# A state-space and mixture-of-experts kernel: states of four channel groups summed side by side, D * u as products with diagonals

## The reference

```
xi, z = split(x @ in_w.T);  u = silu(causal_conv4(xi) + conv_b)
dt, B, C = split(u @ x_w.T, [8, 24])
delta = softplus(dt @ dt_w.T + dt_b);  A = -exp(A_log)          # 256 channels x 16 states
h[t] = h[t-1] * exp(delta[t] * A) + delta[t] * u[t] * B[t]
y[t] = sum over the states of h[t] * C[t]  +  u[t] * D
out = (y * silu(z)) @ out_w.T
```

## Time and profile before

| | us |
|---|---|
| median of three runs (lowest, highest) | 963.63 (962.39, 965.27) |
| the profiled execution's own time | 960.58 |
| its span, first to last instruction | 958.7 |
| DVE busy | 883.0 |
| PE, POOL, ACT busy | 816.3, 801.6, 707.4 |
| mean granted clock of PE | 0.931 of 2.4 GHz |

### The profile page before, as it was taken

One profiled execution on the slowest core, in us unless ns is written; L12 is line 12 of the kernel. 1 busy time (PEld: TensorE's weight loads), 2 busy tenths in 40 slices (PEclk: granted clock), 3 DMA queues, 4 the chain that ended last, 5 costly groups with the idle time before them and its releaser, 6 DMA issues. The chain is left out here.

```text
span 958.7 us, 10740 instructions
## 1 busy us (share of the span) xinstructions
PE 816.3 (85%) x3009; PEld 327.2 (34%) x3009; DVE 883.0 (92%) x628; ACT 707.4 (74%) x1184; POOL 801.6 (84%) x451
## 2 busy tenths in 40 slices
PE   8787887796498998989898998989989899889577
PEld 5323322141133533435233443434434242223122
DVE  4979989998899999999899899998999999998986
ACT  4588774765468899887888889898788968574540
POOL 0468676999999999988798979998798999999993
PEclk9979989898799999999799999989999998889788
DMA  6676254332364647364453655654365444553300
GB/s 210 178 213 160 50 145 97 138 102 70 129 152 154 154 125 184 98 191 116 151 130 102 188 133 173 162 157 103 86 203 133 136 105 130 133 172 74 91 0 12
DMA packets 91452, 125.56 MB, mean 131 GB/s; under 512 B 8057, under 2 KB 62714, under 8 KB 87426
## 3 DMA queue, kind: packets, MB, share of 16 engines
q1 hardware_dynamic: 89346, 120.68, 46.0%
q0 software_dynamic: 2048, 4.20, 1.3%
HBM read 77.53 MB, written 14.29 MB: 96 GB/s over the span
## 5 line engine op out<-in xcount | busy, mean ns | idle before, releaser
L1314 POOL TENSOR_TENSOR hs<-hs,C_rep 128x1024 f32<-128x1024 f32 x250 | 585.0, 2359 | 70.6 <-DVE hs L1116 37.7
L1097 DVE TENSOR_TENSOR in_b<-in_b,B_rep 128x1024 f32<-128x1024 f32 x256 | 300.3, 1217 | 41.2 <-PE in_b L580 41.0
L917 ACT ACTIVATE dA<-delta_rep,A_sb 128x511 f32<-128x511 f32 x512 | 332.9, 713 | 1.7 <-DVE hs L1116 1.2
L604 PE MATMUL y<-hs,cst 128*32 128x512 f32 x1024 | 274.1, 656 | 32.2 <-POOL hs L1314 20.8
L1116 DVE TENSOR_TENSOR_SCAN hs<-dA,in_b 128x1024 f32<-128x1024 f32 x128 | 285.5, 2268 | 8.6 <-ACT dA L917 4.8
L1114 DVE TENSOR_TENSOR_SCAN hs<-dA,in_b 128x1024 f32<-128x1024 f32 x128 | 285.2, 2268 | 2.4 <-PE y L604 1.6
L580 PE MATMUL in_b<-du,cst 128*128 128x512 f32 x256 | 144.2, 646 | 29.8 <-DVE hs L1116 20.5
L604 PEld LDWEIGHTS y<-hs,cst 128*32 128x32 f32 x1024 | 52.5, 115 | 207.1 <-issue 165.5
L541 PE MATMUL front<-xpad,w_in 128*128 128x512 f32 x248 | 120.5, 610 | 2.4 <-ACT xpad L829 1.6
L926 ACT ACT_TABLE_LOAD x71 | 91.1, 1283 | 7.3 <-PE moe L732 4.7
L580 PEld LDWEIGHTS in_b<-du,cst 128*128 128x128 f32 x256 | 43.8, 197 | 96.4 <-issue 93.7
(11 more groups left out here) (144 smaller groups left out, 805.4 us busy)
## 6 DMA issues: line engine op xcount, KB each, us to landing
delta_rep<-tmpA SPq DMA_DIRECT2D x126, 256.0 KB, 4.4
C_rep<-dbc_scratch SPq DMA_DIRECT2D x16, 1024.0 KB, 7.4
B_rep<-dbc_scratch SPq DMA_DIRECT2D x15, 1024.0 KB, 5.2
gu_w<-in_gate_up SPq DMA_DIRECT2D x39, 384.0 KB, 3.3
dn_w<-in_down SPq DMA_DIRECT2D x39, 192.0 KB, 2.5
xs<-sorted_tokens SPq DMA_DIRECT2D x39, 64.0 KB, 3.9
sorted_ffn<-ys SPq DMA_DIRECT2D x39, 64.0 KB, 2.2
sorted_tokens<-up_f SPq DMA_DIRECT2D x9, 256.0 KB, 4.5
```

The lines of the kernel that those rows point to most:

```text
L604: i = e.matmul(Y[c * DD:(c + 1) * DD, :], sel, hs[:, (m + 2 * w + rh) % NH, r * L:(r + 1) * L], start=False, stop=(rh == 1 and r == RH - 1 ...
L917: i = e.activation(dA[:, m // 2 % NA, r * L + 1:(r + 1) * L], src, ACT.Exp, scale=A_sb[:, d, 2 * p + jj, r:r + 1])
L1097: e.tensor_tensor(to, in_b[:, 2 + 2 * odd, :].unsqueeze(1).broadcast_to([P, RH, L]), by, ALU.mult).then_inc(dve_mult, 1)
L1314: e.tensor_tensor(hs[:, m % NH, :], hs[:, m % NH, :], C_rep[:, u % 2, RH * rh:RH * rh + RH, :].rearrange("p r t -> p (r t)"), ALU.mult).th ...
```

## The change

- **Sums.** `sum_states` takes half a unit: four channel groups, each in its own 32 columns of the array, interleaved. A call has 8 products (16 instructions), one for even and one for odd steps, at steps 8i+12 and 8i+13. The ring hs has 13 slots.
- **D * u.** ACT's L899 is gone; PE's `skip` starts the bank Y with a product of a diagonal (`diag_D`, four of them, made by DVE in the head) and u.
- **Decays.** dA has four tiles of half a group; decay m waits for scan m-4. `delta_rep` has five single slots in place of three pairs.
- **dbc** lies in tmpB[:, 1], softplus' buffer; dt_out(v, 1) waits until it is stored.
- **Residual.** xn_in is gone: ACT's `residual` makes x + norm(x) from x_in with 4 activations, and one product adds it.
- **Order.** On every engine pieces are moved within a step or by some steps; one more product with C (step 180) is on DVE.

Before and after, cut to its core:

```diff
-NP = 3
-NA, NH = 3, 10
+NP, NR = 3, 5
+NA, NH = 4, 13
-CLEAR = 4
-WARM, WARM_PAUSE = 24, 7
+CLEAR = 3
+WARM, WARM_PAUSE = 24, 5
-C_ON_DVE = (41, 56, 217, 226, LAST - 2, LAST - 1)
+C_ON_DVE = (41, 56, 180, 217, 226, LAST - 2, LAST - 1)
...
-        dbc = sb("dbc", [NDBC, L])
-        delta_rep = sb("delta_rep", [P, NP, 2, L])
+        dbc = tmpB[0:NDBC, 1, :]
+        delta_rep = sb("delta_rep", [P, NR, L])
-        dA = sb("dA", [P, NA, R * L + 1])
+        dA = sb("dA", [P, NA, RH * L + 1])
...
# PE
+            def skip(i):
+                u, h = divmod(i, 2)
+                e.wait_ge(act_y, i)
+                e.wait_ge(act_xi, i + 1)
+                e.wait_ge(dve_diag, 4)
+                e.matmul(Y[:, :], diag_D[:, 2 * (u % 2) + h, :], xi[:, u % 2, h, :], start=True, stop=False,
+                         skip_group_check=True).then_inc(pe_skip, 1)
-            def sum_states(u, p, rh, groups=(0, 1)):
-                m = NSTEP * u + 4 * p
-                if m and p % 2 == 0 and rh == 0:
-                    e.wait_ge(act_D, 2 * u + p // 2)
+            def sum_states(u, h, rh, groups=(0, 1, 2, 3), signal=True):
+                m = NSTEP * u + 8 * h
                 wait_c(e, m + 2 * groups[-1] + rh)
                 for r in range(RH):
-                    for w in groups:
-                        c = (2 * p + w) % 4
-                        i = e.matmul(Y[c * DD:(c + 1) * DD, :], sel, hs[:, (m + 2 * w + rh) % NH, r * L:(r + 1) * L],
+                    for c in groups:
+                        i = e.matmul(Y[c * DD:(c + 1) * DD, :], sel, hs[:, (m + 2 * c + rh) % NH, r * L:(r + 1) * L],
...
-                for v in fronts(m, -11, -11):
+                for v in fronts(m, -10, -11):
                     x_proj(v)
-                for v in fronts(m, -10, -10):
+                for v in fronts(m, -10, -11):
                     dt_proj(v, 0)
-                for v in fronts(m, -9, -9):
+                for v in fronts(m, -9, -10):
                     dt_proj(v, 1)
-                for b in gathers(m, 6):
+                for b in gathers(m, 7):
                     if b < NB - LATE:
                         final_mm(b)
...
# ACT
+            def residual(b):
+                e.wait_ge(in_base, 16 * (b + 1))
+                for k in range(KB):
+                    o = e.activation(x_in[:, k, :], x_in[:, k, :], ACT.Identity, scale=root1[:, b, k:k + 1],
+                                     bias=shift[:, b, 0, k:k + 1])
+                o.then_inc(act_base, 1)
             def dt_out(v, h):
                 e.wait_ge(pe_dt, 2 * v + h + 1)
+                if h:
+                    e.wait_ge(out_dbc, 16 * (v + 1))
...
-                e.activation(Y[:, :], xi[:, u % 2, h, :], ACT.Copy,
-                             scale=cols[:, 8 + 2 * (u % 2) + h:9 + 2 * (u % 2) + h]).then_inc(act_D, 1)
...
-                if m >= 2 * NA:
-                    e.wait_ge(dve_scan, m - 2 * NA + 1)
+                if m >= NA:
+                    e.wait_ge(dve_scan, m - NA + 1)
...
-                for v in fronts(m, -6, -6):
+                for v in fronts(m, -4, -6):
                     keep_z(v, 1)
# SP
-                for b in gathers(m, 8):
+                for b in gathers(m, 5):
                     if b < NB - LATE:
                         e.wait_ge(act_fin, b + 1)
```

More of the change, by code:

```diff
@@ L64, in ln_step @@
 def ln_step(c, part):
-    return (0, 3, 6, 9, 12, 15, 18, 21)[c] + (-3, 0, 2, 2, 3, 4, 5)[part]
+    return (0, 3, 6, 9, 13, 15, 18, 21)[c] + (-3, 0, 2, 3, 3, 4, 5)[part]
 def norms(m, part):
@@ L679, in tensor_program @@
                 u, s = divmod(m, NSTEP)
+                for i in range(1, 2 * UNITS):
+                    if 8 * i + 8 == m:
+                        skip(i)
+                if m == 0:
+                    z_proj(0, 0)
+                    z_proj(0, 1)
+                for v in fronts(m, -16, -16):
+                    if v > 1:
+                        in_proj(v, 0, 0)
+                for v in fronts(m, -15, -15):
+                    if v == 1:
+                        in_proj(v, 0, 0)
+                    in_proj(v, 0, 1)
+                for v in fronts(m, -14, -14):
+                    in_proj(v, 1, 0)
+                for v in fronts(m, -13, -13):
+                    in_proj(v, 1, 1)
+                for b in turns(m, -18):
+                    turn_x(b)
+                if m >= 12 and m - 12 < LAST - 8 and (m - 12) % 8 == 0:
+                    u2, s2 = divmod(m - 12, NSTEP)
+                    sum_states(u2, s2 // 8, 0)
+                for v in fronts(m, -10, -11):
+                    x_proj(v)
                 if m % 2 and m + 1 < LAST:
@@ L748, in tensor_program @@
+                for v in fronts(m, -10, -11):
+                    dt_proj(v, 0)
+                for v in fronts(m, -9, -10):
+                    dt_proj(v, 1)
+                for v in fronts(m, -8, -8):
+                    z_proj(v, 0)
+                for v in fronts(m, -7, -7):
+                    z_proj(v, 1)
                 for b in range(NB):
@@ L1022, in scalar_program @@
                         silu(v)
-                if m % 8 == 6 and 0 <= m // 8 - 1 < 2 * UNITS - 1:
-                    next_y(m // 8 - 1)
+                if m + LEAD < LAST:
+                    table(EXP_SET)
+                    decay(m + LEAD)
+                for b in turns(m, -20):
+                    norm_two(b)
+                for b in gathers(m, 7):
+                    if b < NB - LATE:
+                        e.wait_ge(pe_fin, b + 1)
+                        e.copy(attn_in[:, b % 2, :, :].rearrange("p k h -> p (k h)"), M[:, :]).then_inc(act_fin, 1)
+                for c in norms(m, 1):
+                    norm_one(c)
                 for v in fronts(m, -6, -6):
@@ L1027, in scalar_program @@
                     softplus(v, 1)
+                for v in fronts(m, -8, -9):
+                    table(EXP_SET)
+                    softplus(v, 0)
+                if m % 8 == 6 and 0 <= m // 8 - 1 < 2 * UNITS - 1:
+                    next_y(m // 8 - 1)
                 for b in range(NB):
@@ L1230, in vector_program @@
             fold_conv(0)
-            e.tensor_scalar(diag_D[:, :], ident, cols[:, 8:9], None, ALU.mult).then_inc(dve_diag, 1)
+            for i in range(4):
+                e.tensor_scalar(diag_D[:, i, :], ident, cols[:, 8 + i:9 + i], None, ALU.mult).then_inc(dve_diag, 1)
             e.wait_ge(in_back, 48)
```

244 lines of the change are left out of this document (104 added, 140 removed).

## The result

The changed kernel takes 933.4 us, the median of four runs (932.21 to 934.74), beside 963.2 us for the kernel before on the same chip: ratio 0.970, 95% interval 0.967 to 0.973. The forecast was 951.6 with a range from 941 to 967. The direction was right, the size was not: the gain is 29.8 us in place of 12, and the time lies outside the range. Some 4 us of the 29.8 come from which executions were profiled: between the two profiled ones, 960.6 and 934.7, the gain is 25.8, and between their spans, 958.7 and 932.5, it is 26.2.

A forecast was written before the change was run, and what follows sets the result against it. The prediction took DVE, busy for 883.0 of 958.7 us, as the bound. Its terms, -15 + 6.3 - 5 - 2.8 + 1.5 + 3 = -12.0 us, gave a span of 946.7 and a forecast of 951.6 us, range 941 to 967.

The forecast's parts named there:

- 280 to 880: waits that go: Units with experts: of DVE's 23.8 us idle, waits behind packed PE stretches, for hs slots and late ACT go, -15 us.
- the new wait: Odd fronts: the spread queues behind a second dt product waiting for ACT; DVE loses 0.9 us seven times, +6.3 us.
- units 14 and 15: Around 880 to 915 us: DVE's idle times of 3.51 and 4.86 us shrink by 3 and 2, -5 us.
- 32 to 280 us: unit 3, the first two units: Unit 3: DVE's decay wait of 2.80 us goes, -2.8 us; the first two units, 12 us idle, stay as they are.
- one more C product on DVE: Step 180: one more product with C lies on the bound, DVE, +1.5 us.
- clock: Whole kernel: PE with less work runs 30 us more at half clock, +3 us, bounds 0 and +13.
- ring of decays: ACT: decay m waits for scan m-4, no longer m-6; costs 0 us, upper end +6.
- nearly 9 us: 280 to 880 us: the rest of DVE's 23.8 us idle, following half clock or a late decay, stays.
- (b): Fronts: the wait only moves, 967 us for all 14 fronts; 0.14 for about 961, odd fronts alone with less won.
- (c): Every unit: PE's queue thins so much that half clock comes everywhere; slower, about 970 us, chance 0.12.
- (d): Sum calls: the sums don't run four abreast, 137 us of PE work return and spreads are late; 966 us, chance 0.04.
- Rival (a): PE is early everywhere, neither the new wait nor the clock costs anything: -25 us, 938, chance 0.08.

The follow-up runs named there:

- run 7: The changed kernel with a semaphore wait inside each full sum call, groups 2 and 3 starting only after groups 0 and 1 end: 971.3 us, ratio 1.010.
- run 10: The changed kernel with the semaphore wait between halves only in the sum calls of odd steps: 954.5 us, ratio 0.993.
- run 1: The changed kernel with the sums in pairs again, two channel groups per call at the steps of before, all else kept: 964.7 us, ratio 1.005.
- run 3: The changed kernel with D * u written by ACT again and PE's skip left out: 944.9 us, ratio 0.983.
- run 8: The changed kernel with ACT's program in the sequence within a step of the kernel before, step numbers as changed: 941.8 us, ratio 0.980.
- run 5: The changed kernel with the spread at the top of its step on PE, ahead of projections, sums and x_proj: 942.1 us, ratio 0.978.
- run 4: The changed kernel with dt_proj(v, 1) of odd v one step later, behind the spread: 929.3 us, ratio 0.967.
- run 2: The changed kernel with each call's products of groups 0 and 1 written before those of 2 and 3, without a wait: 935.5 us, ratio 0.974.

## Why the prediction was wrong

The forecast's terms, beside what the traces of before and after and the runs gave:

| step | forecast | measured |
|---|---|---|
| 280 to 880: waits that go, and the new one | -15, +6.3 | -15.9 together |
| units 14 and 15 | -5 | -5.4 |
| 32 to 280 us: unit 3, the first two units | -2.8, 0 | about -5 |
| one more C product on DVE | +1.5 | +1.6 in its line, 0 in DVE's busy time |
| clock | +3 | open; at most 5.7, within the first row |
| ring of decays | 0 (to +6) | +2.6 with pairs |

Of the 14.2 us between -12.0 and -26.2, 7.2 lie in the first row.

**Right.** PE's work: 137 us for the sums, found 141.1; 35 for D * u, found 40.2; in sum 110 less. The page has only 72 less. PE was busy for 156.3 us at half clock in place of 108.4, and half of those 48 us, an estimate, is stretch. Four abreast, 1.92 us for a call. The estimate from the 2.38 of the Trainium skill (TensorE: Matmul & The Clock Gate, Measured speedup vs the span model), 174 us, was too high; 274.1 / 141.1 is 1.94 over two abreast. The place in unit 10 (2.72 us) went. The end of the program: the 3.51 and 4.86 us of the earlier trace rows are gone, and 2.29 and 0.65 us for sums and spreads came:

```profile
882.49 3.64 PE L610 MATMUL y<-hs,cst 128*32 128x512 f32 x16 [7.45 <-POOL hs L1343]
...
886.19 2.29 DVE L1136 TENSOR_TENSOR_SCAN hs<-dA,in_b 128x1024 f32<-128x1024 f32 x1 [2.29 <-PE y L610]
```

In unit 3 the decay wait of 2.80 us is gone, but ACT's wait for POOL is still there (7.55 us), and DVE waits at 262.59 for a sum instead:

```profile
228.32 2.29 DVE L1136 TENSOR_TENSOR_SCAN hs<-dA,in_b 128x1024 f32<-128x1024 f32 x1 [3.50 <-PE y L610]
...
256.62 0.58 ACT L869 COPY zs<-front 128x512 f32<-128x512 f32 x1 [7.55 <-POOL yg L1334]
...
262.59 2.29 DVE L1136 TENSOR_TENSOR_SCAN hs<-dA,in_b 128x1024 f32<-128x1024 f32 x1 [4.27 <-PE y L610]
```

So -2.8 was right as to that wait alone. Unit 3 as a whole gained nothing, since the two waits for sums took its place, and the gain of this stretch lies in the first two units and in spreads.

**The step that failed** is the sum for 280 to 880 us. I sorted the 23.8 us idle by the place in which DVE stood, and let "nearly 9 us" stay, as following half clock or a late decay. They did not stay. Of the waits that the kernel before had in these units only a decay wait of 0.33 us is left. The 7.9 us are 3.03 us at a new place in unit 9, the new wait (1.31 and 1.34), 0.84 at 861.76 and 0.54 in unit 5. DVE's wait for spreads went to 15.9 us, not to 25. The reasoning behind the sum was the sentence that none of PE's work is on DVE's path by itself, that what counts is where it sits. Runs 7 and 10 say otherwise: with the call's place unchanged, each us added to the sums costs a third of a us, from the first to the last. A reading that fits is that PE's queue is in order and nearly full, so that a delay is handed on to the next spread until a gap takes it up; run 1, where the whole loss is in the wait for spreads, fits it, and in runs 7 and 10 the ring of states has a share that no run parts. An average price per us would have come nearer than the list of places, but it is no constant: for the 110 us of the forecast the 0.18 to 0.35 seen here give 20 to 39 us, an estimate, beside the 26.2.

**The second failure** is of terms put at nothing. ACT was called 6 us lighter and not the bound (found 7.6, 707.4 to 699.8), and its relief went into no term. Moving D * u off ACT gives 11.5 us (run 3, the clock with it) and its new sequence 8.4 (run 8). The spread's move behind the projections, the first sum and x_proj of its step, which is part of the change and stood in no term of the sum, gives 8.7 (run 5). These do not add: each was measured by taking it out of the finished kernel, and with the sums in pairs D * u gives 3.4.

**The new wait** was priced at 6.3 us. The trace shows it in two of seven fronts, 1.31 and 1.34 us, and run 4 gave 2.5 to 5. In the other fronts no wait of DVE shows there; in unit 14 PE waited 3.96 us for ACT at the same product (832.56) and DVE lost nothing.

**The clock.** The mean fell from 0.931 to 0.891. Half clock went from 126.6 us to 199.1 us in 33 stretches, 73 us more and not the 30 assumed; the sum over them, with DVE's busy time third:

```profile
sum 199.14, PE 156.27 PEld 62.28 DVE 178.87 ACT 131.87 POOL 173.63; mean PE 4.74 PEld 1.89 DVE 5.42 ACT 4.00 POOL 5.26
```

DVE is idle in them for 20.3 us, of which 4.6 are a stretch behind its last scan: 15.7 beside 17.9 before, with half as much again of half clock. The prediction read idle time at half clock as its price; by that reading it should have grown with the half clock, and it did not. The clock was lower where PE had more idle time (188 us in place of 142), which agrees with the Trainium skill's rule of idle gaps between bursts (TensorE: Matmul & The Clock Gate, Why this matters for your kernels). The time didn't rise with it, but three places look like a price. One, of at most 3.03 us, is a projection of 3.78 us at half clock, behind a wait for ACT, ahead of a late spread.

```profile
545.35 3.78 PE L540 MATMUL front<-xpad,w_in 128*128 128x512 f32 x4 [3.16 <-ACT xi L863]
...
554.27 2.36 DVE L1117 TENSOR_TENSOR in_b<-in_b,B_rep 128x1024 f32<-128x1024 f32 x2 [3.03 <-PE in_b L579]
```

The others are the two places of the new wait, in units 10 and 12:

```profile
726.32 2.07 PE L572 MATMUL front<-tmpB,w_dt 8*128 8x512 f32 x2 [4.26 <-ACT tmpB L896]
...
728.32 2.08 PE L579 MATMUL in_b<-du,cst 128*128 128x512 f32 x2
...
730.43 2.36 DVE L1117 TENSOR_TENSOR in_b<-in_b,B_rep 128x1024 f32<-128x1024 f32 x2 [1.34 <-PE in_b L579]
```

A dt product and a spread at full clock take 1.12 and 1.02 us. At these rows' half clock they take 2.0 us more together, which is more than the 1.31 and 1.34 us that DVE lost: at full clock the new wait would not have been there, an estimate. So of the waits from 280 to 880 us at most 5.7 us are the clock's. It was not varied by itself, and its price stays open; rivals (b), (c) and (d) did not come. Rival (a), 938, was the nearest, and had 0.08: too little, since it was the case in which PE is early everywhere. Also open: the half of run 8's 8.4 us that its profiled execution does not show, and whether D * u, priced alone, would be worth as much under another sequence of ACT.

## What to carry to other kernels

Where an in-order engine that is nearly full feeds the bound, price its work by a share of a us for each us (0.18 to 0.35 for the sums, here), beside the list of places where the bound now waits. Put a product that must wait behind those of its step that can run already: here that was worth 8.7 us. Ask of every engine that feeds the one you relieve what its own relief is worth. And a ring is to be judged in the form that will use it: three slots were worth 0.5 to 5 us under one layout of the calls, and one of them 32 under another. A ring that an in-order engine waits at holds up all that stands behind, so look at who waits for that engine's other work.

## What the runs showed of the hardware

- Eight fp32 products of 128 x 32 by 512 columns, in four column groups of the array, take 1.92 us; four products in two groups take 1.91 us. Four abreast cost nothing over two. At half clock the call takes 3.64 us (at 882.49).
- The order of the products in the call does not matter: groups 0 and 1 first, then 2 and 3, took 1.94 us (run 2). With a semaphore between the halves the same 16 instructions took 3.89 us (run 7).
- A mean clock of 0.891 in place of 0.931, with 73 us more at half clock, stood beside 72 us less busy time of PE and a gain of 3%; from 280 to 880 us three waits of DVE, 5.7 us together, stand behind products at half clock.
